# Four order tables of a fused decoder's attention rewritten: scan and C product of a side state-space model, the next context's normalising and turning, and the spacing of the key maxima

## The chip, the cores and the metric

The kernel runs on 1 core of one Trainium2 chip. Times are device microseconds (us) of one execution; the lower the better. The core's engines run side by side and meet at semaphores: TensorE (PE in the profile), VectorE (DVE), ScalarE (ACT), GpSimd (POOL) and SyncE (SP), which here only issues DMAs.

## The reference

A decoder layer on `x` (4 batches of 512 rows, 256 wide) with a context `ctx_1024` (4 batches of 1601 rows, 256 wide), in three steps, each followed by a layer norm over the sum with its input:

```python
# step 1, a Mamba block: 512 inner channels, 16 states each
dt = softplus(dt @ W_dt.T + b_dt)
dA = exp(dt[..., None] * A)
dBx = dt[..., None] * Bm[:, :, None, :] * xs[..., None]
def step(h, inputs):
    dA_t, dBx_t, C_t = inputs
    h = dA_t * h + dBx_t                      # the scan over 512 positions
    return h, einsum('bdn,bn->bd', h, C_t)    # the C product
out = (ys + xs * D) * silu(z) @ W_out.T
# step 2, cross attention: 16 heads of 64, keys and values from the context and the rows
xn, ln = layer_norm(ctx_1024), layer_norm(x)
q = ln @ Wq;  k, v = split(concat([xn, ln]) @ Wkv)       # 1601 + 512 = 2113 keys
out = softmax(q k^T / 8) v @ Wout
# step 3, a mixture of 8 experts (2 of them per row) and 2 shared ones
```

## The kernel before

Three blocks run one after the other: `mamba`, `attention`, `experts`. The change touches `attention` alone, about 450 to 2909 us of the profiled span. `mamba` finishes step 1 for one batch only. For the other three it keeps in DRAM what the scans need: `dtu` (dt and dt*x of 128 channels), `bc` (one row of B and one of C for each state), `y` and `z`. Their scans are done beside the attention of the batch before.

**Heads and slots.** `attention` goes through 4 batches of 16 heads, 64 heads `g`, and each head through KT = 17 slots `kt` of 128 keys. A slot on PE is two matmuls for the scores (L1246, L1247), then whatever the table gives it, then the product with the values of three slots before (LAG = 3, L1259). ACT takes the exponential of each slot's scores (L904). There are two banks of scores, so the engines walk through the slots nearly in step.

**The table.** `beside(g)` (L466) writes, for each head and slot, a list of letters with what is done beside it. PE, DVE, ACT and POOL each walk the same table in the same order and do their part of each letter; nothing but the semaphores holds an engine back. In the order in which a slot's list is filled:

- D and H: the scans. A batch has NU = 64 units, one for each block of 128 channels and state. Unit `u` has its D in slot `int(u * 2.85)`, counted through the batch's heads, and its H some slots `later`. At D, ACT makes the decays (L882) and POOL `dbx` = dtu * B (`times_b`, L795). At H, DVE scans (L992), and POOL multiplies with C (`times_c`, L802) and adds to `y` (L806).
- Q, K, V: projections; a head pair's Q and five K in slots 0 to 5 of its odd head (`g % 4` is 1 or 3); V in slots 6 to 15 of every fourth head.
- O: the output projection of the head before, in slots 6 to 9.
- P and G (head 12 of a batch): the output of the state-space block of the next batch (PE L1210) and the variance of its norm; J (head 13): that norm applied (DVE L1073).
- S, A, L, N, T: the next batch's context. S takes statistics of 13 tiles of 128 rows (head 12, DVE), A sums them in two halves, L does the same for the 512 rows of `x` (DVE L966 to L971), POOL makes the two `rstd` (L779, L782). N(i) normalises a pair of tiles on DVE (L983). T(i) turns it: PE transposes (L1137), ACT scales and shifts (L852) and copies (L856), DVE subtracts (L1008). `PREP` has 10 such pieces: six pairs and a single of context, a pair and two singles of `x`.
- X and M: the maxima of the next head's scores. X has 17 pieces, one matmul of 512 keys each (L1188) and one DVE reduction (L1042), in two banks: PE may be two pieces ahead of DVE. M turns the row of maxima (L1199) in slot 15.

**Buffers of the scans.** `dbx`, `decay`, `state` and `bc` have two buffers, by the unit's number `n`; `seen` has one. SP walks the slots too, with its loads in a fixed order. The load of `bc` for unit n waits until the C product of unit n - 2 has read its buffer:

```python
            def load_bc(b, u):
                n = unit(b, u)
                if n >= 2:
                    sp.wait_ge(seen_ready, n - 1)
                sp.dma_start(bc[:, n % 2]...,
                             KEPT["bc"][BATCHES[b], u % NS].partition_broadcast(P)).then_inc(bc_loaded[n % 2], 16)
```

It is 512 KB. The other loads of SP (weights, `wo`, the copies `k_one` of the keys) stand between these in the same queue.

Of the kernel before, what the change touches and what calls it, by code (L numbers as in the profile page):

```python
# [438 lines left out]
H, DH, LC = 16, 64, 1601  # L439
# [6 lines left out]
KT = -(-KV // P)  # L446
KL = KV - (KT - 1) * P
CTX_T = -(-LC // P)
# [10 lines left out]
NX = TT * (len(KC) - 1) + 1  # L459
# [6 lines left out]
def beside(g):  # L466

    at = {kt: [] for kt in range(KT)}
    b, h = divmod(g, H)
    j, more, following = g % HG, g + 1 < NH, b + 1 < B
    if following:
        for u in range(NU):
            for kind, later in (("D", 0), ("H", 2)):
                if divmod(int(u * U_STEP) + later, KT)[0] == h:
                    at[(int(u * U_STEP) + later) % KT].append((kind, b + 1, u))  # L480
    if j == 0:
        for i in range(V_EARLY, len(VB)):
            at[i - V_EARLY].append(("V", g // HG, i))
    if j % 2 == 1 and more:
        at[0].append(("Q", (g + 1) // 2, 0))
        for i in range(len(KC)):
            at[1 + i].append(("K", (g + 1) // 2, i))
    if j == HG - 1 and more:
        for i in range(V_EARLY):
            at[6 + 2 * i if i < 5 else 15].append(("V", (g + 1) // HG, i))  # L490
    if g > 0:
        for t in range(TT):
            at[6 + t].append(("O", g - 1, t))
    if following and h == 12:
        for t in range(TT):
            at[10 + t].append(("P", b + 1, t))
        at[15].append(("G", b + 1, 0))
        for t in range(CTX_T):
            at[t].append(("S", b + 1, t))
    if following and h == 13:  # L500
        at[3].append(("J", b + 1, 0))
        for i in range(2):
            at[7 + 4 * i].append(("A", b + 1, i))
        at[14].append(("L", b + 1, 0))
    if following and h == 14:
        for i in range(len(PREP)):
            at[(3 * i) // 2].append(("N", b + 1, i))
            at[1 + (3 * i) // 2].append(("T", b + 1, i))
    if b > 0 and h == 0:
        at[12].append(("E", b - 1, 0))  # L510
        at[16].append(("F", b - 1, 0))
    if more:
        for i in range(NX):
            at[i * 14 // NX if j % 2 == 0 else 3 + i * 11 // NX].append(("X", g + 1, i))
        at[15].append(("M", g + 1, 0))
    return at


BESIDE = [beside(g) for g in range(NH)]
BEFORE = [("S", 0, t) for t in range(CTX_T)] + [("A", 0, i) for i in range(2)] + [("L", 0, 0)]  # L520
BEFORE += [("N", 0, i) for i in range(3)]
# [9 lines left out]
POW = {x: i for i, x in enumerate(x for x in MADE if x[0] in "EGL" or x[0] == "A" and x[2] == 1)}  # L531


def attention(nc, ctx_rows, g1, b1, g2, b2, wq, wkv, wo, x1):
    w_dram = nc.dram_tensor("a_w_split", (NG, P, 6 * KD * GW), F32, kind="Internal").ap()

    with ExitStack() as ctx:
# [3 lines left out]
        def sem(name):  # L541
            return ctx.enter_context(nc.semaphore(name))
# [76 lines left out]
        rstd_ready = sem("a_rstd_ready")  # L619
# [33 lines left out]
        def x1_rows(b, t):  # L653
            return x1[:, BATCHES[b] * TT + t]
# [273 lines left out]
        def _(dve):  # L928
# [44 lines left out]
            def normalised(what):  # L973
                b, i = what[1:]
                t, n, r, col = PREP[i]
                if i == 0:
                    dve.wait_ge(rstd_ready, POW["L", b, 0] + 1)
                for j in range(t, t + n):
                    if j < CTX_T:
                        src = dst = rows[0:r, j]  # L980
                    else:
                        src, dst = x1_rows(b, j - CTX_T), lat[:, j - CTX_T]
                    s = nc.vector.tensor_scalar(dst, src, mv[0:r, j, 0:1], rstd[0:r, j:j + 1], ALU.subtract, ALU.mult)  # L983
                s.then_inc(rows_ready, 1)
# [92 lines left out]
            def make(what):  # L1077
                kind = what[0]
                if kind in "QKV":
                    low(what)  # L1080
                elif kind == "X":
                    row_max(what[1], what[2])
                elif kind == "O":
                    add_out(what)
                elif kind == "S":
                    row_stats(what)
                elif kind == "A":
                    row_sums(what)
                elif kind == "N":
                    normalised(what)  # L1090
                elif kind == "T":
                    low_rows(what)
                elif kind == "H":
                    scan(*what[1:])
                elif kind == "P":
                    add_mamba(what)
                elif kind == "L":
                    latent_sums(what[1])
                elif kind == "G":
                    norm_var(what[1], [("P", what[1], t) for t in (TT - 2, TT - 1)])  # L1100
                elif kind == "J":
                    norm_rows(what[1], ("G", what[1], 0))
                elif kind == "E":
                    norm_var(what[1], [("O", what[1] * H + H - 1, t) for t in (TT - 2, TT - 1)])
                elif kind == "F":
                    norm_rows(what[1], ("E", what[1], 0))
# [893 lines left out]
```

## Time and profile before

| | |
|---|---|
| median of 3 runs | 3380.14 us (3371.8 to 3387.71) |
| profiled execution | 3382.36 us, its span 3380.6 us |
| mean granted TensorE clock | 0.951 |
| busy: PE, DVE, ACT, POOL | 3017.8, 1940.5, 1351.0, 964.5 us |
| the attention's first head starts | about 461 us |
| first heads of batches 1, 2, 3 | about 1083, 1707, 2336 us |

The chain of work that ended last reaches back only to about 2909 us, into the experts, so it says nothing of the attention. There one reads stretches: the fourth batch has the same heads as the others without the scans and without a next context, so that its heads, beside those of another batch, show what these cost. The times at which heads begin are the starts of the score matmuls (L1247).

### The profile page before, as it was taken

Reading aid. Unit: us, or ns where it says so; the run is one execution under the profiler, and the core shown is the slowest. Engines: PE = TensorE matmul, PEld = TensorE weight load, DVE = VectorE, ACT = ScalarE, POOL = GpSimd, SP = SyncE. Lnnn points to the kernel's source line nnn. Section 1 sums busy time; section 2 is a strip of 40 time slices with the busy share of each in tenths; the row PEclk is TensorE's granted clock in tenths of the full one; section 3 lists DMA queues with packets and bytes.
Section 4 is the critical chain, followed back from the end, with each engine's and each line's share of the span. In section 5 each row is a group of like instructions: output and inputs, shape, how many; then the busy total and the mean of one; then the engine's idle time right before and its main releaser. Section 6 shows DMA issues by size and latency. Waiting matters only on the chain. (4 is left out here: it accounts for less than half of the span.)

```text
span 3380.6 us, 34291 instructions
## 1 busy us (share of the span) xinstructions
PE 3017.8 (89%) x11694; PEld 1872.9 (55%) x11694; DVE 1940.5 (57%) x3342; ACT 1351.0 (40%) x2320; POOL 964.5 (29%) x760
## 2 busy tenths in 40 slices
PE   6746289999999999999899999989999999799976
PEld 2212155665656565656566565656566665576655
DVE  4699466666555766665576666555555454442225
ACT  4532134445344445443544544344433434211111
POOL 1044336566101656540046666000000000102131
PEclk8878589999999999999999999999999999799997
DMA  3200344344112434231123433110111100411121
GB/s 114 89 0 0 130 127 129 103 126 132 39 35 63 129 100 134 95 104 34 51 86 125 126 104 115 33 35 14 35 22 33 42 13 13 156 55 54 50 59 37
DMA packets 90914, 248.57 MB, mean 74 GB/s; under 512 B 10660, under 2 KB 44584, under 8 KB 83064
## 3 DMA queue, kind: packets, MB, share of 16 engines
q1 hardware_dynamic: 86760, 237.04, 22.8%
q0 software_dynamic: 3408, 9.31, 1.0%
q8 instruction: 97, 1.59, 0.2%
q14 instruction: 73, 0.60, 0.1%
q10 hardware_dynamic: 576, 0.04, 0.0%
HBM read 183.34 MB, written 28.38 MB: 63 GB/s over the span
## 5 line engine op out<-in xcount | busy, mean ns | idle before, releaser
L904 ACT ACTIVATE a_p<-a_st 128x512 f32<-128x512 f32 (+1 forms) x1088 | 649.2, 597 | 1214.2 <-PE a_st L1247 1205.3
L1259 PE MATMUL a_o<-a_p,a_vals 128*65 128x512 f32 (+1 forms) x2176 | 1118.4, 596 | 0.0
L1042 DVE TENSOR_REDUCE a_maxes<-a_mx 128x1 f32<-128x512 f32 x1024 | 673.3, 682 | 112.3 <-PE a_mx L1188 106.0
L1246 PE MATMUL a_st<-a_qd,a_kodd 128*128 128x512 f32 (+1 forms) x544 | 434.7, 799 | 0.0
L1246 PE MATMUL a_st<-a_qd,a_keven 128*128 128x512 f32 (+1 forms) x544 | 434.6, 799 | 0.0
L1247 PE MATMUL a_st<-a_qm,a_kone 65*128 65x512 f32 (+1 forms) x1088 | 431.8, 397 | 0.0
L802 POOL TENSOR_TENSOR a_shared<-a_shared,a_bc 128x512 f32<-128x512 f32 x192 | 245.5, 1279 | 477.7 <-DVE a_shared L992 477.7
L1259 PEld LDWEIGHTS a_o<-a_p,a_vals 128*65 128x65 f32 (+1 forms) x2176 | 288.6, 137 | 124.5 <-issue 2.7
L1247 PEld LDWEIGHTS a_st<-a_qm,a_kone 65*128 65x128 f32 (+1 forms) x1088 | 204.1, 188 | 265.5 <-issue 265.4
L992 DVE TENSOR_TENSOR_SCAN a_shared<-a_shared 128x512 f32<-128x512 f32 x192 | 234.3, 1220 | 178.8 <-POOL a_shared L795 129.6
L795 POOL TENSOR_TENSOR a_shared<-a_dtu,a_bc 128x512 f32<-128x512 f32 x192 | 245.1, 1276 | 197.7 <-DMA a_bc<-m_kept_bc 197.7
L784 POOL TENSOR_TENSOR a_erstd<-a_emv,a_half 128x4 f32<-128x4 f32 x7 | 7.1, 1014 | 919.8 <-DVE a_emv L1068 919.6
L1144 PE MATMUL a_ring<-a_kvh,a_wt 128*128 128x512 f32 (+1 forms) x768 | 228.6, 380 | 26.7 <-POOL a_wt L820 20.7
L806 POOL TENSOR_TENSOR a_y<-a_y,a_shared 128x512 f32<-128x512 f32 x192 | 245.0, 1276 | 15.3
L1188 PE MATMUL a_mx<-a_keven,a_qd 128*128 128x512 f32 x512 | 215.3, 471 | 32.9 <-DVE a_maxes L1042 28.6
L1188 PE MATMUL a_mx<-a_kodd,a_qd 128*128 128x512 f32 x512 | 218.8, 452 | 28.9 <-DVE a_maxes L1042 28.3
L1035 DVE COPY a_vals<-a_ring 128x512 f32<-128x512 f32 (+2 forms) x160 | 97.6, 610 | 235.8 <-PE a_ring L1144 234.9
L1246 PEld LDWEIGHTS a_st<-a_qd,a_kodd 128*128 128x128 f32 (+1 forms) x544 | 101.7, 187 | 160.2 <-issue 118.7
L1246 PEld LDWEIGHTS a_st<-a_qd,a_keven 128*128 128x128 f32 (+1 forms) x544 | 101.7, 187 | 159.2 <-issue 103.9
L1144 PEld LDWEIGHTS a_ring<-a_kvh,a_wt 128*128 128x128 f32 x768 | 142.3, 192 | 67.1 <-issue 21.1
L1523 ACT ACTIVATE e_silu<-e_h 128x512 f32<-128x512 f32 x71 | 42.4, 597 | 334.5 <-PE e_h L1865 185.5
L1651 DVE TENSOR_TENSOR e_gate<-e_silu,e_h 128x512 f32<-128x512 f32 x71 | 48.7, 686 | 220.5 <-ACT e_silu L1523 217.3
(242 smaller groups left out, 4451.6 us busy)
## 6 DMA issues: line engine op xcount, KB each, us to landing
a_bc<-m_kept_bc SPq DMA_DIRECT2D x192, 512.0 KB, 3.7
a_wt<-a_w_split SPq DMA_DIRECT2D x15, 1536.0 KB, 9.4
a_kone<-a_keven SPq DMA_DIRECT2D x32, 528.5 KB, 5.0
a_kone<-a_kodd SPq DMA_DIRECT2D x32, 528.5 KB, 5.5
e_wall<-in_w_t_dram SPq DMA_DIRECT2D x27, 512.0 KB, 5.2
a_shared<-in_ctx_dram SPq DMA_DIRECT2D x4, 1536.0 KB
a_w_split<-a_wt SPq DMA_DIRECT2D x4, 1536.0 KB, 6.5
a_dtu<-m_kept_dtu SPq DMA_DIRECT2D x12, 512.0 KB, 4.9
```

Of the source, the lines that this page charges most:

```text
L795: nc.gpsimd.tensor_tensor(dbx[:, n % 2], dtu[:, c % 2, 1], bc[:, n % 2, 0], ALU.mult).then_inc(dbx_ready, 1)
L802: nc.gpsimd.tensor_tensor(seen, state[:, n % 2], bc[:, n % 2, 1], ALU.mult).then_inc(seen_ready, 1)
L806: nc.gpsimd.tensor_tensor(y[:, c], y[:, c], seen, ALU.add).then_inc(y_added, 1)
L904: nc.scalar.activation(p[0:r, s % 4], st[0:r, s % 2], ACT.Exp, scale=SCALE).then_inc(exp_done, 1)
L992: nc.vector.tensor_tensor_scan(state[:, n % 2], decay[:, n % 2], dbx[:, n % 2], 0.0, ALU.mult, ALU.add).then_inc(scanned, 1)
L1035: o = nc.vector.tensor_copy(vals[0:r, t * HG:(t + w) * HG, 0:DH], made)
L1042: nc.vector.reduce_max(maxes[:, c, t:t + 1], mx[:, i % 2], AX_X).then_inc(mx_max, 1)
L1144: mm = nc.tensor.matmul(out, x(k), y(k), start=(j == 0), stop=(j == len(terms) - 1))
L1188: mm = nc.tensor.matmul(mx[:, i % 2], qd[of(g)][:, t * P:(t + 1) * P], kk[:, c * 512:(c + 1) * 512], start=True, stop=True)
L1246: nc.tensor.matmul(st[0:r, s % 2], keys_of(g)[:, kt * P:kt * P + r], qd[of(g)][:], start=True, stop=False)
L1247: nc.tensor.matmul(st[0:r, s % 2], k_one[g % 2][0:DH + 1, kt * P:kt * P + r], qm[of(g)][0:DH + 1, :], start=False, stop=True).then_inc(st_ ...
L1259: nc.tensor.matmul(ps_o[0:DH + 1, g % 2], vals[0:r, kt * HG + j, :], p[0:r, s % 4], start=(kt == 0), stop=(kt == KT - 1)).then_inc(pv_done, 1)
```

## The change

Four things, all in the tables. H comes four slots behind D, where it was two. A's halves move from slots 7 and 11 of head 13 to slot 10 of head 12 and slot 0 of head 13, L from slot 14 to slot 13. N and T, all in head 14 before, are spread over heads 13 and 14, each T two slots behind its N, where it was one. In odd heads the 17 pieces of X are spaced wider at first and end one slot later.

```diff
-            for kind, later in (("D", 0), ("H", 2)):
+            for kind, later in (("D", 0), ("H", 4)):
                 if divmod(int(u * U_STEP) + later, KT)[0] == h:
                     at[(int(u * U_STEP) + later) % KT].append((kind, b + 1, u))
...
+        at[10].append(("A", b + 1, 0))
     if following and h == 13:
+        at[0].append(("A", b + 1, 1))
         at[3].append(("J", b + 1, 0))
-        for i in range(2):
-            at[7 + 4 * i].append(("A", b + 1, i))
-        at[14].append(("L", b + 1, 0))
-    if following and h == 14:
+        at[13].append(("L", b + 1, 0))
+    if following and h in (13, 14):
         for i in range(len(PREP)):
-            at[(3 * i) // 2].append(("N", b + 1, i))
-            at[1 + (3 * i) // 2].append(("T", b + 1, i))
+            for kind, slot in (("N", 6 + 2 * i), ("T", 8 + 2 * i)):
+                if i >= CTX_T // 2 + 1:
+                    slot += 1
+                if slot // KT == h - 13:
+                    at[slot % KT].append((kind, b + 1, i))
...
-            at[i * 14 // NX if j % 2 == 0 else 3 + i * 11 // NX].append(("X", g + 1, i))
+            at[i * 14 // NX if j % 2 == 0 else 3 + i if i < 2 else 5 + (i - 2) * 2 // 3].append(("X", g + 1, i))
...
                 if i == 0:
+                    dve.wait_ge(rstd_ready, POW["A", b, 1] + 1)
+                if t == CTX_T:
                     dve.wait_ge(rstd_ready, POW["L", b, 0] + 1)
```

The first place is POOL's order at the start of a batch's scans; in the kernel before, where L795 is `times_b`, L802 and L806 are `times_c`:

```order
L795 TENSOR_TENSOR a_shared<-a_dtu,a_bc 128x512 [waits a_bc_loaded0,a_dtu_loaded0,a_turned_low]
L802 TENSOR_TENSOR a_shared<-a_shared,a_bc 128x512 [waits a_scanned]
L806 TENSOR_TENSOR a_y<-a_y,a_shared 128x512 [waits a_seen_ready,a_y_loaded]
L795 TENSOR_TENSOR a_shared<-a_dtu,a_bc 128x512 [waits a_bc_loaded1,a_turned_low]
L802 TENSOR_TENSOR a_shared<-a_shared,a_bc 128x512 [waits a_y_added,a_scanned]
L806 TENSOR_TENSOR a_y<-a_y,a_shared 128x512 [waits a_seen_ready]
L795 TENSOR_TENSOR a_shared<-a_dtu,a_bc 128x512 [waits a_scanned,a_bc_loaded0]
```

The same start in the changed kernel, where the three lines are L798, L805 and L809:

```order
L798 TENSOR_TENSOR a_shared<-a_dtu,a_bc 128x512 [waits a_bc_loaded0,a_dtu_loaded0,a_turned_low]
L798 TENSOR_TENSOR a_shared<-a_dtu,a_bc 128x512 [waits a_bc_loaded1,a_turned_low]
L805 TENSOR_TENSOR a_shared<-a_shared,a_bc 128x512 [waits a_scanned]
L809 TENSOR_TENSOR a_y<-a_y,a_shared 128x512 [waits a_seen_ready,a_y_loaded]
L798 TENSOR_TENSOR a_shared<-a_dtu,a_bc 128x512 [waits a_scanned,a_bc_loaded0]
L805 TENSOR_TENSOR a_shared<-a_shared,a_bc 128x512 [waits a_y_added,a_scanned]
L809 TENSOR_TENSOR a_y<-a_y,a_shared 128x512 [waits a_seen_ready]
L798 TENSOR_TENSOR a_shared<-a_dtu,a_bc 128x512 [waits a_scanned,a_bc_loaded1]
```

Before, the three operations of one unit stand together, B(0) C(0) B(1) C(1) B(2). Now it is B(0) B(1) C(0) B(2) C(1) B(3): the C product of unit n - 2, which lets SP load `bc` for unit n, stands directly ahead of that unit's product with B.

The second place is DVE's order at the next context's pieces, early in head 14, in the kernel before (L983 is N, L1008 the end of T, L1042 an X):

```order
L1042 TENSOR_REDUCE a_maxes<-a_mx 128x1 [waits a_mx_full] x2
L1008 TENSOR_TENSOR a_kvl<-a_shared,a_kvh 128x2x256 [waits a_turned_high]
L983 TENSOR_SCALAR a_shared<-a_shared,a_mv,a_rstd 128x256 x2
L1042 TENSOR_REDUCE a_maxes<-a_mx 128x1 [waits a_mx_full]
L1008 TENSOR_TENSOR a_kvl<-a_shared,a_kvh 128x2x256 [waits a_turned_high]
L1042 TENSOR_REDUCE a_maxes<-a_mx 128x1 [waits a_mx_full]
L983 TENSOR_SCALAR a_shared<-a_shared,a_mv,a_rstd 128x256 x2
```

DVE's order in slots 10 to 15 of head 13 in the changed kernel, where N is L988, the end of T is L1013, X is L1047 and L1049, and L969 to L974 are the statistics of the rows of `x` (L):

```order
L1013 TENSOR_TENSOR a_kvl<-a_shared,a_kvh 128x2x256 [waits a_turned_high]
L988 TENSOR_SCALAR a_shared<-a_shared,a_mv,a_rstd 128x256 x2
L1047 TENSOR_REDUCE a_maxes<-a_mx 128x1 [waits a_mx_full]
L969 BN_STATS a_stats<-rows 128x6 x4
L972 BN_AGGR a_mv<-a_stats 128x2 [waits a_dve_step]
L972 BN_AGGR a_mv<-a_stats 128x2 x3
L974 TENSOR_SCALAR a_mv<-a_mv 128x4 [waits a_dve_step]
L1047 TENSOR_REDUCE a_maxes<-a_mx 128x1 [waits a_mx_full] x2
L1013 TENSOR_TENSOR a_kvl<-a_shared,a_kvh 128x2x256 [waits a_turned_high]
L988 TENSOR_SCALAR a_shared<-a_shared,a_mv,a_rstd 128x256 x2
L1049 TENSOR_REDUCE a_maxes<-a_mx 128x4 [waits a_mx_full]
```

Before, each N stood right behind the end of the T of the pair before it and one slot ahead of its own T on PE. Now a slot or two with X lie between, and the last maxima of head 13 stand behind L and behind a T and an N.

## Rows read from the trace of the kernel before

**Rows 1.** The page: busy time, share of the span and instructions of each engine.

```profile
PE 3017.8 (89%) x11694; PEld 1872.9 (55%) x11694; DVE 1940.5 (57%) x3342; ACT 1351.0 (40%) x2320; POOL 964.5 (29%) x760
```

**Rows 2.** Windows, heads 0-9, batches 1, 3: us, busy PE PEld DVE ACT POOL, clock, DMA.

```profile
1082.80:1457.70 374.90, 362.06 (x1415) 221.32 (x1414) 255.88 (x416) 185.01 (x320) 227.60 (x181) 1.00 0.37 113
2335.60:2696.50 360.90, 357.83 (x1415) 223.04 (x1414) 186.83 (x357) 149.20 (x260) 1.01 (x1) 1.00 0.12 31
```

**Rows 3.** Page, costliest groups: times_c on POOL and the scan on DVE.

```profile
L802 POOL TENSOR_TENSOR a_shared<-a_shared,a_bc 128x512 f32<-128x512 f32 x192 | 245.5, 1279 | 477.7 <-DVE a_shared L992 477.7
...
L992 DVE TENSOR_TENSOR_SCAN a_shared<-a_shared 128x512 f32<-128x512 f32 x192 | 234.3, 1220 | 178.8 <-POOL a_shared L795 129.6
```

**Rows 4.** Line L992, one window for each batch's 64 scans: first and last start.

```profile
L992 DVE TENSOR_TENSOR_SCAN a_shared<-a_shared x64: 1211/1223/1227, 465.7 to 856.0; 128x512 f32<-128x512 f32 x64
...
L992 DVE TENSOR_TENSOR_SCAN a_shared<-a_shared x64: 1208/1223/1226, 1088.1 to 1483.4; 128x512 f32<-128x512 f32 x64
...
L992 DVE TENSOR_TENSOR_SCAN a_shared<-a_shared x64: 1208/1223/1226, 1712.1 to 2109.0; 128x512 f32<-128x512 f32 x64
```

**Rows 5.** Timeline of POOL: start, length, line, idle before.

```profile
630.10 1.28 POOL L795 TENSOR_TENSOR a_shared<-a_dtu,a_bc 128x512 f32<-128x512 f32 x1
632.77 1.28 POOL L802 TENSOR_TENSOR a_shared<-a_shared,a_bc 128x512 f32<-128x512 f32 x1 [1.39 <-DVE a_shared L992]
...
635.37 1.26 POOL L795 TENSOR_TENSOR a_shared<-a_dtu,a_bc 128x512 f32<-128x512 f32 x1
```

**Rows 6.** Page, DMA issues: KB each, median us to landing.

```profile
a_bc<-m_kept_bc SPq DMA_DIRECT2D x192, 512.0 KB, 3.7
```

**Rows 7.** Tile a_bc: loads issued at 478.9, at 839.2, and all of batch 0's scans.

```profile
DMA to landing us min/median/max: 5.3/5.3/5.3
...
DMA to landing us min/median/max: 6.1/6.1/6.1
...
DMA to landing us min/median/max: 3.3/3.7/10.2
```

**Rows 8.** Timeline of SP near the 62nd unit: start, length of issuing.

```profile
828.71 0.32 SPq L690 DMA_DIRECT2D a_bc<-m_kept_bc  x1
829.07 0.43 SPq L736 DMA_DIRECT2D a_wt<-a_w_split  x1
...
833.97 5.58 SPq L690 DMA_DIRECT2D a_bc<-m_kept_bc  x2
```

**Rows 9.** Timeline of POOL at the 62nd unit.

```profile
844.21 1.26 POOL L795 TENSOR_TENSOR a_shared<-a_dtu,a_bc 128x512 f32<-128x512 f32 x1 [3.65 <-DMA a_bc<-m_kept_bc]
```

**Rows 10.** Waits of the whole span: PE for the maxima.

```profile
PEld a_mx L1188 <- DVE a_maxes L1042: 88.0, 123, 3.8
...
PE a_mx L1188 <- DVE a_maxes L1042: 56.9, 89, 3.4
```

**Rows 11.** Waits in slots 3 to 5 of head 11 of batch 3.

```profile
PEld a_mx L1188 <- DVE a_maxes L1042: 1.1, 2, 0.7
...
PE a_mx L1188 <- DVE a_maxes L1042: 0.5, 2, 0.3
```

**Rows 12.** Waits in head 14 of batch 0.

```profile
PE a_ring L1137 <- DVE a_shared L983: 7.4, 8, 1.8
```

**Rows 13.** Windows: heads 13, 14 of batch 0, 13 of batch 1, 13, 14 of batch 3.

```profile
951.10:993.30 42.20, 40.42 (x138) 24.57 (x137) 25.60 (x67) 18.64 (x33) 3.43 (x2) 0.92 0.19 57
993.30:1036.50 43.20, 34.70 (x136) 19.04 (x135) 23.26 (x51) 25.46 (x49) 0.00 (x0) 1.00 0.06 13
1578.50:1617.30 38.80, 37.03 (x137) 22.55 (x136) 25.61 (x67) 18.63 (x33) 3.44 (x2) 1.00 0.20 62
2804.00:2841.90 37.90, 37.29 (x137) 22.67 (x137) 20.67 (x38) 18.63 (x33) 0.00 (x0) 1.00 0.07 15
2841.90:2870.70 28.80, 28.80 (x101) 16.45 (x100) 13.62 (x26) 11.21 (x19) 0.00 (x0) 1.00 0.09 19
```

**Rows 14.** Line L966 in head 13 of batch 0.

```profile
L966 DVE BATCH_NORM_STATS2 a_stats<-rows x4: 408/408/416, 988.5 to 989.5; 128x6 f32<-128x256 f32 x4
```

## The prediction

> **What bounds the kernel now.** I began with the page's busy times: PE is busy 89% of the span, more than any other [rows 1]. The chain that ended last lies in the experts, which the change leaves alone, so for the attention I compared stretches. Heads 0 to 9 take 374.9 us in batch 1, with scans beside them, and 360.9 us in batch 3, without; PE is busy for all but 3.1 us of the latter [rows 2]. So PE sets the pace, and the scans cost 14.0 us in these ten heads. Without scans a slot takes 360.9 / 170 = 2.12 us, and the 2.85 slots from one unit to the next 6.05 us.
>
> The scans have a ring of their own. POOL waits 477.7 us for the scan, 192 times, and DVE 129.6 us for POOL [rows 3]. The reader is to see how the ring closes where it is tight: POOL multiplies with B from 630.10 to 631.38, waits 1.39 us while DVE scans, multiplies with C at 632.77, adds, and begins with the next B at 635.37 [rows 5]. One unit takes 5.27 us there, less than 6.05, so the ring holds PE up only in heads whose slots are short. Over whole batches the scans start 390.3, 395.3 and 396.9 us apart from first to last [rows 4], 6.20 to 6.30 us a unit.
>
> **Scan and C product four slots behind.** No instruction is added or removed; the ring is cut open. DVE no longer scans right behind POOL's B: the scan of unit n stands behind B(n + 1) on POOL, so the 1.39 us in which POOL waits for it can go. That is the gain meant, at most the 14.0 us above, or 15 a batch with the units that fall behind head 9 (64 units at 2.85 slots end in head 10).
>
> Now what comes late next. `bc` has two buffers; SP loads unit n's when C(n - 2) has read it. Before, POOL did C(n - 2), add, B(n - 1), C(n - 1), add and then B(n), so a load had over 6 us. Now C(n - 2), its add and B(n) are neighbours: a load has 1.28 us of cover, the add. POOL is in order, so C(n - 1) stands behind the waiting B(n), and C(n - 1) is what lets SP load for unit n + 1. This is a new ring, one unit long, with a DMA in it: C, load, B, C, load, B. DVE's next scan waits for B, the maxima (X) stand behind that scan on DVE, and PE, two maxima ahead at most, waits for them; ACT's decays, and the exponentials behind them, wait for the scan too. The wait is not new in kind. It shows once in batch 0: a load issued at 833.97 [rows 8] lands 10.2 us later, the longest of batch 0 [rows 7], and POOL, which would have gone on at 840.6, sits idle for 3.65 us and starts B at 844.21, 0.07 us behind the landing [rows 9].
>
> Its length: C 1.28 and B 1.28 [rows 3, 5], 0.14 us between the operations (0.07 behind a landing as just seen, 0.07 for the two others, C to SP's issue and B to C), and the load. The page gives 3.7 us in the median for 512 KB [rows 6], and the shortest in batch 0 is 3.3 [rows 7]. A ring adds up means, not medians: of 62 loads in batch 0 (from unit 2 on), 14 land after 4.3 us or more, the first 5.3 (issued at 478.9), the last 6.1 (issued at 839.2), 5.81 on average, and 48 after 3.62 on average [rows 7]: together 4.11. Batches 1 and 2 give the same to 0.02. The long ones have a cause that stays: SP issues key copies and weights right behind a `bc` load, as at 829.07 behind 828.71 [rows 8]. So a unit takes 2.56 + 0.14 + 4.11 = 6.81 us, above today's 6.20 to 6.30.
>
> This is a floor, whatever PE does: from scan 0 to scan 63 it is scan 1.22, 0.07, C 1.28, load 4.14 with its issue, 0.07 to B(2), 61 units of 6.81, and B(63) with its hand-over 1.37, in all 423.6 us. Against 390.3, 395.3 and 396.9 that is +33.3, +28.3 and +26.7, together +88. At the end of each batch PE may be two light slots (28.8 / 17 = 1.7 us each [rows 13]), some 3 us, ahead of the waiting scan, which I count as not yet so today: -9. Sum **+79**. Both ends: with every load at 3.62 the stretch is 393.2 us, the sum about 0 and with the lead -10; with a mean of 4.4 it is 18 us a batch more than taken, +132. I take 4.11, since the companions of the long loads stay in the queue where they are.
>
> **A rule against a row.** The rows say 3.3 at best and 3.7 in the median for this load [rows 6, 7]. The Trainium skill, DMA: Bandwidth & Descriptors (Anatomy of one DMA) fits a DMA as about 2.0 us fixed plus bytes / 436 GB/s, fitted on GpSimd's path, which for 512 KB would be an estimate of 3.2 us and a unit of 5.9: below the pace of PE, and the ring would cost nothing. This case's trace does not agree, with 3.7. The same page (Rules for kernel authors) says to issue early and wait late; this edit brings issue and wait closer, and by that rule it speaks against the change.
>
> **Maxima spaced wider in odd heads.** PE waits for maxima 88.0 + 56.9 us in the whole span (weight loads and matmuls) [rows 10]; part is the scans' doing. In slots 3 to 5 of an odd head, where the keys' subtractions crowd DVE, it is 1.1 + 0.5 = 1.6 us [rows 11]. Two maxima in slots 3 and 4 each become one, with two in slot 5. There the second has to wait for the maximum of slot 4, which stands behind the fourth key chunk on DVE: of the 1.6 I count half, 0.8 us. It counts only where POOL does not set the pace: heads 11, 13, 15 in three batches and seven heads of batch 3, 16 heads, **-13**. Bounds: 0, and 1.6 each, -26. The last maximum, a slot later, still lies a slot ahead of M.
>
> **The next context.** Head 14 takes 43.2 us against 28.8 in batch 3, head 13 42.2 and 38.8 against 37.9 [rows 13]. Of this, PE waits 7.4 us in head 14 for the normalised rows, 8 times [rows 12]; the rest are transposes, which are only moved, and DVE waits. With T two slots behind N these waits should go: -22 in three batches. In batch 0 head 13 shows a clock of 0.92 and 3.4 us more than in batch 1 at 1.00: one dip to the 1.2 GHz level behind the stall at J. Fewer maxima beside J may spare it in some batches: -3. Costs: L, 4 statistics of 0.41 us and what follows, about 2.1 us on DVE [rows 14], now stands ahead of two maxima in slot 13, and the last maximum and M behind it, and behind the end of a T, which waits for ACT; five T now fall in the odd head 13, whose DVE has more to do. I count 4 us a batch, +12. The halves of A go where DVE is busy 25.6 of 42.2 us [rows 13]: nothing, and some 1 us if that cover were gone. Sum **-13**. Bounds -30 and +5.
>
> **Sum.** 79 - 13 - 13 = +53, on the profiled execution's own 3382.4 us: 3435. The median of the runs is 2.2 us lower, so **3433**.
>
> **Rivals.**
> - *The POOL ring with the load in it decides*, as above: +53. For it: the buffers and the order; against it: the load has only been seen while POOL was busy. Mean loads of 4.0 to 4.35 give 3413 to 3477. Chance 0.72.
> - *The long loads fall into slack* and only the usual 3.62 counts: -10 - 26 = -36, 3344. For it: where slots take over 2.4 us (6.81 / 2.85), POOL catches up; against it: light ones use this up again, since the ring is over the average pace. 0.10. Between this and the first, near 3380, 0.06. The time turns at a mean load of about 3.83 us, where the scans' term is +26.
> - *The edit does what it seems made for*: the scans' stalls vanish, 15 us a batch, and the maxima help in all 31 odd heads at 0.8, -45 - 25 - 13 = -83, 3299. That needs a unit under 6.05 us, a load under 3.35, which the fastest alone reach; the page cited above would have it so. 0.04.
> - *Slower still*: loads grow when SP's other transfers bunch behind the later issue, or POOL waits for scans as well. A mean of 4.6 gives +90 more, 3523. 0.08.
>
> **Range and chances.** 3390 to 3480 holds the first case and edges of its neighbours, and leaves out about 2 in 10. What differs by under 0.5% (17 us) counts as the same. Faster 0.14, same 0.06, slower 0.80.
>
> **What would show it.** In the changed profile POOL's `times_b` should wait for `a_bc` often, over 100 times and over 400 us in total, and its wait for the scan should be small. The scans' first and last starts should lie about 424 us apart. Heads 0 to 9 should be slower than 374.9 us, near 400. Heads 11 and 15 should be 0.8 us shorter, 13 and 14 together a few us. PE's wait for L983's successor should be near nothing. I am wrong if the load takes under 3.8 us on average, or if POOL finds `bc` there already.

## The result, and the profile after

| | before | after |
|---|---|---|
| median | 3381.02 us (4 runs) | 3462.21 us (4 runs, 3461.65 to 3465.95) |
| ratio | | 1.0234 [1.0216, 1.0251] |
| span of the profiled execution | 3380.6 us | 3460.8 us |
| mean granted TensorE clock | 0.951 | 0.941 |

The change costs 81 us; 53 were forecast. In the changed kernel the product with B is L798, the product with C L805, the addition L809, the scan L997, N L988, the end of T L1013, X L1193 on PE and L1047 on DVE. The page's busy times, to be read beside [rows 1]:

```profile
PE 3038.6 (88%) x11690; PEld 1885.5 (54%) x11694; DVE 2034.7 (59%) x3342; ACT 1351.4 (39%) x2320; POOL 1040.8 (30%) x760
...
L798 POOL TENSOR_TENSOR a_shared<-a_dtu,a_bc 128x512 f32<-128x512 f32 x192 | 253.5, 1321 | 585.7 <-DMA a_bc<-m_kept_bc 565.8
L997 DVE TENSOR_TENSOR_SCAN a_shared<-a_shared 128x512 f32<-128x512 f32 x192 | 330.9, 1723 | 113.8 <-POOL a_shared L798 68.8
...
L809 POOL TENSOR_TENSOR a_y<-a_y,a_shared 128x512 f32<-128x512 f32 x192 | 313.4, 1632 | 15.3
...
L805 POOL TENSOR_TENSOR a_shared<-a_shared,a_bc 128x512 f32<-128x512 f32 x192 | 244.8, 1275 | 99.6 <-DVE a_shared L997 99.2
```

Two things are to be seen. POOL's idle time has changed sides: it waited 477.7 us for scans [rows 3], and now waits 99.2 us for scans and 565.8 us for `bc`. In each kernel three long waits of either kind stand at the start of a batch. Inside the batches POOL waited 418 us for scans and 18 for `bc`; now it waits 31 for scans and 394 for `bc`. And with no instruction added, DVE is busy 94 us longer and POOL 76: the scan takes 1.72 us instead of 1.22, the addition 1.63 where POOL's other operations take 1.28 to 1.32. The first was forecast, the second not. How often POOL waited, in the view of waits (total us, times, longest):

```profile
POOL a_shared L798 <- DMA a_bc<-m_kept_bc: 565.8, 179, 71.5
...
POOL a_shared L805 <- DVE a_shared L997: 99.2, 25, 25.4
```

Before, the wait for `bc` was 197.7 us in 12 times, nine of them inside the batches. The scans of the three batches, one window each, with the number, min/median/max in ns, and first and last start, against [rows 4]:

```profile
L997 DVE TENSOR_TENSOR_SCAN a_shared<-a_shared x64: 1210/1830/2303, 468.6 to 888.9; 128x512 f32<-128x512 f32 x64
...
L997 DVE TENSOR_TENSOR_SCAN a_shared<-a_shared x64: 1210/1598/2319, 1122.2 to 1540.7; 128x512 f32<-128x512 f32 x64
...
L997 DVE TENSOR_TENSOR_SCAN a_shared<-a_shared x64: 1210/1715/2243, 1775.6 to 2196.2; 128x512 f32<-128x512 f32 x64
```

They are 420.3, 418.5 and 420.6 us apart, where the ring was worked out at 423.6: 30.0, 23.2 and 23.7 more than before, 76.9 in all. The windows of heads 0 to 9 of batches 1 and 3, heads 13 and 14 of batch 0 and head 13 of batch 3, with the columns of [rows 2, 13]:

```profile
1112.30:1506.80 394.50, 370.77 (x1416) 226.79 (x1415) 282.03 (x416) 185.61 (x320) 242.36 (x177) 0.97 0.34 106
2419.60:2780.20 360.60, 355.68 (x1416) 223.06 (x1415) 187.24 (x357) 149.20 (x260) 1.01 (x1) 1.00 0.12 31
980.80:1032.30 51.50, 42.00 (x158) 25.11 (x157) 30.31 (x73) 25.34 (x47) 3.44 (x2) 0.97 0.17 49
1032.30:1066.00 33.70, 31.57 (x115) 17.42 (x114) 18.20 (x39) 18.29 (x36) 0.00 (x0) 1.00 0.06 13
2887.60:2925.30 37.70, 36.72 (x137) 22.65 (x136) 20.78 (x38) 18.64 (x33) 0.00 (x0) 1.00 0.07 15
```

Heads 0 to 9 with scans take 394.5 us instead of 374.9; without them nothing moved. Head 13 has become 9.3 us longer and head 14 9.5 shorter. By the starts of the score matmuls, summed over heads:

| us | batch 0 | batch 1 | batch 2 | sum of the differences | forecast |
|---|---|---|---|---|---|
| heads 0 to 10, before | 404.4 | 410.1 | 411.7 | | |
| heads 0 to 10, after | 433.9 | 434.8 | 436.8 | +79.3 | +79 |
| heads 11, 15 and all of batch 3 | | | | 0 | -13 with head 13 |
| head 13, before / after | 42.1 / 51.5 | 38.8 / 53.1 | 42.1 / 51.5 | +33.1 | |
| head 14, before / after | 43.2 / 33.7 | 43.2 / 33.8 | 43.2 / 33.8 | -28.3 | |
| heads 13 and 14 | | | | +4.8 | -13 |

Batch 3 begins at 2419.6 us instead of 2335.6, 84 later; what follows gives 3 back.

### The profile page after: what moved, and what is told of

Same layout as the page of the kernel before. It is cut to its first block and busy times, and to the rows that moved or that the text cites. A ratio compares the mean times of both kernels' runs of the same rounds, so it can differ in the third digit from the quotient of the medians.

```text
span 3460.8 us, 34287 instructions
## 1 busy us (share of the span) xinstructions
PE 3038.6 (88%) x11690; PEld 1885.5 (54%) x11694; DVE 2034.7 (59%) x3342; ACT 1351.4 (39%) x2320; POOL 1040.8 (30%) x760
## 5 line engine op out<-in xcount | busy, mean ns | idle before, releaser
L1264 PE MATMUL a_o<-a_p,a_vals 128*65 128x512 f32 (+1 forms) x2176 | 1136.3, 604 | 0.0
L1047 DVE TENSOR_REDUCE a_maxes<-a_mx 128x1 f32<-128x512 f32 x1024 | 676.1, 682 | 126.0 <-PE a_mx L1193 120.5
L798 POOL TENSOR_TENSOR a_shared<-a_dtu,a_bc 128x512 f32<-128x512 f32 x192 | 253.5, 1321 | 585.7 <-DMA a_bc<-m_kept_bc 565.8
L997 DVE TENSOR_TENSOR_SCAN a_shared<-a_shared 128x512 f32<-128x512 f32 x192 | 330.9, 1723 | 113.8 <-POOL a_shared L798 68.8
L809 POOL TENSOR_TENSOR a_y<-a_y,a_shared 128x512 f32<-128x512 f32 x192 | 313.4, 1632 | 15.3
L1193 PE MATMUL a_mx<-a_keven,a_qd 128*128 128x512 f32 x512 | 223.3, 472 | 68.7 <-DVE a_maxes L1047 68.7
L805 POOL TENSOR_TENSOR a_shared<-a_shared,a_bc 128x512 f32<-128x512 f32 x192 | 244.8, 1275 | 99.6 <-DVE a_shared L997 99.2
L1193 PE MATMUL a_mx<-a_kodd,a_qd 128*128 128x512 f32 x512 | 223.8, 463 | 41.9 <-DVE a_maxes L1047 41.6
L1226 PE MATMUL a_ring<-a_wo,a_osb 65*128 65x257 f32 x512 | 158.3, 392 | 22.9 <-DVE rows L1061 22.2
L1149 PE MATMUL a_ring<-a_wt,a_kvh 128*128 128x256 f32 (+1 forms) x1088 | 175.4, 283 | 0.0
```

Source lines behind the costliest of these rows:

```text
L798: nc.gpsimd.tensor_tensor(dbx[:, n % 2], dtu[:, c % 2, 1], bc[:, n % 2, 0], ALU.mult).then_inc(dbx_ready, 1)
L805: nc.gpsimd.tensor_tensor(seen, state[:, n % 2], bc[:, n % 2, 1], ALU.mult).then_inc(seen_ready, 1)
L809: nc.gpsimd.tensor_tensor(y[:, c], y[:, c], seen, ALU.add).then_inc(y_added, 1)
L997: nc.vector.tensor_tensor_scan(state[:, n % 2], decay[:, n % 2], dbx[:, n % 2], 0.0, ALU.mult, ALU.add).then_inc(scanned, 1)
L1047: nc.vector.reduce_max(maxes[:, c, t:t + 1], mx[:, i % 2], AX_X).then_inc(mx_max, 1)
L1149: mm = nc.tensor.matmul(out, x(k), y(k), start=(j == 0), stop=(j == len(terms) - 1))
```

## The experiments

The theory: the loss is POOL's ring with the load of `bc` in it, and what closes it is two buffers of `bc`. The rivals: the distance of H from D as such; scans and POOL's products slowing each other; heads 13 and 14. Each kernel but one, which ran once, was timed beside the kernel before on the same chip. That kernel's median was 3379.2 to 3382.9 us in these sets, so a difference between kernels of two sets is good to some 4 us.

**A third buffer of `bc` in the changed kernel.** Nothing else is touched: the load waits for the C product of unit n - 3.

```diff
-        bc = sb("a_bc", [P, 2, 2, S])
+        bc = sb("a_bc", [P, 3, 2, S])
...
-                if n >= 2:
-                    sp.wait_ge(seen_ready, n - 1)
-                sp.dma_start(bc[:, n % 2]...
+                if n >= 3:
+                    sp.wait_ge(seen_ready, n - 2)
+                sp.dma_start(bc[:, n % 3]...
```

> The changed kernel with three buffers for bc instead of two: the load for unit n waits for the C product of unit n - 3, so that a whole unit of POOL's work lies between that product and the B product that needs the load. Theory 1 (a ring of C product, load and B product on POOL sets the pace): POOL's 565.8 us of waiting for a_bc, 179 times, shrink to the three batch starts, heads 0 to 10 of a batch fall from 434 to 437 us to under 410, and the kernel takes 3345 us, between 3320 and 3375. Theory 2 (scan and POOL's products slow one another when they run at once, 1.72 us for a scan instead of 1.22 in the changed kernel, and that alone makes it slow): nothing of the overlap is taken away, and it stays within 20 us of 3462.

Measured: 3346.36 us, 0.9891 [0.9876, 0.9905] of before, 116 us below the changed kernel. The waits of POOL and the window of heads 0 to 9 of batch 1:

```profile
POOL a_shared L805 <- DVE a_shared L997: 404.4, 134, 25.9
POOL a_shared L798 <- DMA a_bc<-m_kept_bc: 197.0, 16, 70.5
```

```profile
1072.20:1438.80 366.60, 357.48 (x1415) 221.90 (x1414) 267.77 (x416) 185.18 (x320) 236.01 (x179) 1.00 0.38 118
```

The waits for `bc` fall from 179 to 16 (inside the batches from 394 us to 27), and the ten heads from 394.5 to 366.6 us, 8 below the kernel before and 6 above the heads without scans. The order on POOL and DVE is the changed one; so the two buffers are what makes the order dear. Scans and POOL's products still run side by side (a scan takes 1.44 us on average), so their overlap is not what made the loss.

**The scans' table alone, on the kernel before.**

```diff
-            for kind, later in (("D", 0), ("H", 2)):
+            for kind, later in (("D", 0), ("H", 4)):
```

> The kernel before with H four slots behind D and nothing else changed. The prediction's term is +79: 3382 + 79 = 3461 by theory 1, between 3440 and 3480, with the scans' first and last starts about 420 us apart in each batch. If the other edits matter for it, it lies elsewhere: were the loss that of the context pieces and the maxima, this kernel would be at or under 3400.

Measured: 3460.85 us, 1.0222 [1.0207, 1.0237]. The one number makes 78 of the 81 us (the median of before was 3382.93 beside it); the other edits together make about nothing. Its POOL:

```profile
POOL a_shared L795 <- DMA a_bc<-m_kept_bc: 571.9, 178, 75.8
```

**Three slots instead of two or four**, again on the kernel before (`("H", 3)`).

> The kernel before with H three slots behind D. In about six of seven units POOL's order is still B(n) C(n), in the others B(n + 1) stands ahead of C(n); the scan is one slot later in all. Theory 1 (the order on POOL decides, with two bc buffers): near the kernel before, 3370 to 3395. Rival (the distance in slots decides: whatever is late grows with it): half way to the 3461 of four slots, near 3420.

Measured: 3373.23 us, 0.9974 [0.9959, 0.9989].

```profile
POOL a_shared L802 <- DVE a_shared L992: 414.6, 166, 22.4
POOL a_shared L795 <- DMA a_bc<-m_kept_bc: 244.0, 37, 75.8
```

D comes every 2.85 slots. At three slots H falls behind the next D only where that D comes after two slots instead of three, about one unit in seven; POOL waits for `bc` 37 times. At four slots it falls behind always. So it is not the distance that costs, but that on POOL the order B(n), C(n - 1) has taken the place of C(n - 1), B(n).

**The next context alone**, on the kernel before: A, L, N and T as in the change, nothing else.

> The kernel before with only the A, L, N and T pieces in their new slots. The prediction's term was -13. The profile of the changed kernel shows head 13 at 51.5 to 53.1 us (38.8 to 42.1 before) and head 14 at 33.7 (43.2 before), which is +5 for three batches: 3387 by that reading, 3369 by the prediction. If the loss in head 13 came from scans that ran late, head 13 would be near 45 here and the time near 3365; there are no scans in head 13, so I expect 51 to 53 us again.

Measured: 3388.61 us (10 runs), 1.0016 [1.0005, 1.0027], +5.7. Head 13 takes 51.5, 54.2, 51.5 us and head 14 33.7 to 33.8, as in the changed kernel. The gain in one head is lost in the other.

**The maxima's spacing alone**, on the kernel before.

> The kernel before with only the maxima of odd heads spaced wider. The prediction's term was -13, and -25 where POOL does not set the pace. The changed kernel's profile shows odd heads of batch 3 at 37.8 and 46.3 us as before, so that the wait in slots 3 to 5 has only moved to slot 5 (3.71 us instead of 2.65). By that reading the time is within 5 us of 3381; by the prediction 3356 to 3368.

Measured: 3375.34 us (10 runs), 0.9978 [0.9969, 0.9987], -7.6. The heads that show the spacing undisturbed, the odd ones of batch 3, became shorter by about 0.1 us at most (37.8 and 46.3). The rest is scattered: head 13 takes 39.3, 39.2, 40.9 for 42.1, 38.8, 42.1, which is mostly the dip of the granted clock that batches 0 and 2 had there. So the interval lies below 1, but by another way than the one that I priced.

**A third buffer in the kernel before.** This asks how much of the 116 us is the ring that the change made, and how much a third buffer brings in any order. The edit is that of the first experiment.

> The kernel before with three buffers for bc and nothing else: the control of e1_bc3. In the order B(n) C(n) a load has over 6 us of cover already, and the ring of 5.27 us per unit (B product, scan, C product, add) has no load in it. Theory 1: within 10 us of 3383, the one long wait near the 62nd unit of each batch gone at most. If a third buffer helped for another reason than the ring of the changed kernel, this kernel would come down as e1_bc3 did, by 30 us and more.

Measured: 3355.48 us, 0.9930 [0.9912, 0.9947], -24.5, where next to nothing was expected. Its POOL waits, and the windows of its heads 10 and 13 of batch 0:

```profile
POOL a_shared L802 <- DVE a_shared L992: 477.0, 192, 21.3
POOL a_shared L795 <- DMA a_bc<-m_kept_bc: 180.0, 3, 75.7
```

```profile
829.70:861.30 31.60, 29.56 (x101) 16.17 (x100) 18.85 (x31) 13.54 (x23) 19.94 (x16) 1.00 0.30 80
946.90:985.70 38.80, 37.04 (x138) 22.58 (x137) 25.62 (x67) 18.64 (x33) 3.44 (x2) 1.00 0.21 62
```

The 12 waits for `bc` of the kernel before are now 3, and those 3 are the ones ahead of a batch. What is gone is nine waits, 17.7 us in all, one or two a batch of them longer than 1 us, as the 3.65 us behind the load of 10.2 us [rows 7, 9], and what followed. Head by head, up to head 14 of the last batch, the granted clock is 1.00, the level of 2.4 GHz, where head 10 of every batch, head 13 of two and head 2 of one had shown 0.92 to 0.95; head 10 takes 31.6 us for 35.3, head 13 of batch 0 38.8 for 42.2 [rows 13]. Of the 26 us between the two profiles 18.5 lie in heads 0 to 10 and 6.6 in head 13, where POOL waits for no load: its dip of the clock varies between the batches of one kernel (0.92 in two, 1.00 in the third), and that the buffer took it away is not shown. Of the 116 us, then, some 25 come in the order of before too; the other 90 are the change's. And with three buffers the changed kernel (0.9891 [0.9876, 0.9905]) is faster than the kernel before (0.9930 [0.9912, 0.9947]): taken together, the changed tables do bring something, about 12 us, once the loads have cover.

**Half the load, in the changed kernel.** Only the B row is loaded, 256 KB; the C product multiplies with B's row, so this kernel leaves C out of its result.

```diff
-                sp.dma_start(bc[:, n % 2].rearrange("p i s -> p (i s)"),
-                             KEPT["bc"][BATCHES[b], u % NS].partition_broadcast(P))...
+                sp.dma_start(bc[:, n % 2, 0],
+                             KEPT["bc"][BATCHES[b], u % NS, 0:S].partition_broadcast(P))...
...
-                nc.gpsimd.tensor_tensor(seen, state[:, n % 2], bc[:, n % 2, 1], ALU.mult)...
+                nc.gpsimd.tensor_tensor(seen, state[:, n % 2], bc[:, n % 2, 0], ALU.mult)...
```

> The changed kernel with bc loads of 256 KB: only the row of B is loaded, and the C product multiplies with that row too, so the C product leaves out the row of C. Order, buffers and instructions are the same; only the load in the ring is shorter. Theory 1: a unit is 2.70 us plus the load. The load of 512 KB took 3.92 us on average; should 256 KB take 3.2, a unit is 5.9 us, under PE's 6.05, and the time falls by 61 units x 3 batches x 0.6 us and somewhat more, to 3350 to 3380. Theory 2 (scan and POOL's products slow one another): the overlap stays, and with it 3440 to 3462.

Measured: 3424.76 us, 1.0131 [1.0112, 1.0151]. A miss in size: -37 against the changed kernel, where -80 to -110 was expected.

```profile
DMA to landing us min/median/max: 3.0/3.2/8.7
```

```profile
POOL a_shared L798 <- DMA a_bc<-m_kept_bc: 495.2, 177, 69.3
```

```profile
POOL a_shared L805 <- DVE a_shared L997: 137.9, 44, 26.6
```

Half the bytes took only 0.5 us off the median (3.7 before) and 0.43 off the mean, 3.48. The ring is then 2.70 + 3.48 = 6.18 us, still above the 6.05 of the slots alone. And units came 6.43 to 6.55 us apart. Added up over the 186 units of the ring, the loads took 80 us less; the products with B took 13 us more (they stretch where a scan runs beside them); and POOL, inside the batches, waited 67 us for scans instead of 31. The ring is confirmed, but it was not a lever of 1:1: what the loads gave back went in part to the next thing to come late, the scan.

**POOL's two other operations cut to copies, in the changed kernel.** The C product becomes a copy of the state, the addition a copy; this leaves the product and the sum over states out. It ran once, so its time has no interval.

```diff
-                nc.gpsimd.tensor_tensor(seen, state[:, n % 2], bc[:, n % 2, 1], ALU.mult)...
+                nc.gpsimd.tensor_copy(seen, state[:, n % 2])...
...
-                nc.gpsimd.tensor_tensor(y[:, c], y[:, c], seen, ALU.add)...
+                nc.gpsimd.tensor_copy(y[:, c], seen)...
```

> The changed kernel with POOL's two operations behind the scan made copies of one input: the C product is left out (seen is a copy of the state) and the sum over states too (y is a copy of seen). A look at durations alone. In the changed kernel a scan takes 1.22 us alone and 2.1 us beside C product and add, while the add behind it takes 2.1 us instead of 1.28. If the two engines take turns at a way into SBUF only when POOL reads two inputs, scans beside the copies take 1.22 us; if any operation of POOL does it, they stay at 1.7 us and more. I expect the former to hold in part: the mean scan under 1.5 us.

Measured: 3414.43 us. The page's groups:

```profile
L997 DVE TENSOR_TENSOR_SCAN a_shared<-a_shared 128x512 f32<-128x512 f32 x192 | 267.4, 1393 | 80.7 <-POOL a_shared L798 40.4 <-issue 39.1
L809 POOL COPY a_y<-a_shared 128x512 f32<-128x512 f32 x192 | 160.2, 834 | 11.9
L805 POOL COPY a_shared<-a_shared 128x512 f32<-128x512 f32 x192 | 117.3, 611 | 161.3 <-DVE a_shared L997 161.2
```

The scan's mean falls from 1.72 to 1.39 us, but does not return to 1.22: beside the copies a scan takes 1.50 on average, and alone 1.22 (beside a product with B, which is still there, also 1.50). The copy into `y` takes 0.83 on average, 0.62 with no scan beside it. So operations of one input slow the scan too, for a shorter time. The ring is 0.67 us shorter here as well, so that the 48 us below the changed kernel are no price of the overlap alone.

**The next context, cut another way**, on the kernel before: N alone goes a slot earlier, the first to slot 16 of head 13; all T stay in head 14.

```diff
+        at[16].append(("N", b + 1, 0))
     if following and h == 14:
...
-            at[(3 * i) // 2].append(("N", b + 1, i))
+            if i > 0:
+                at[(3 * i) // 2 - 1].append(("N", b + 1, i))
```

> The kernel before with the context pieces turned in head 14 as before, T in its old slots, and only N moved one slot ahead, so that it stands two slots or more before its T. A, J and L stay. If the loss of the changed kernel's head 13 comes from five T in a head whose DVE is full (each T on DVE waits for ACT, and the maxima behind it), and the gain of its head 14 from N being early, then head 13 stays at 38.8 to 42.1 us and head 14 falls from 43.2 us by most of the 7.4 us for which PE waits for N: to 36 to 38 us. Time 3360 to 3370. If N early does nothing, head 14 stays at 43 and the time at 3383.

Measured: 3366.49 us, 0.9964 [0.9950, 0.9978], -13.5. Head 14 takes 37.4 us for 43.2, head 13 40.4 in every batch (38.8 to 42.1 before).

**What these point to, together**: the changed kernel with three buffers of `bc`, H four slots behind, the wider maxima, and the context of the last experiment in place of the change's.

> What the experiments point to, together: three bc buffers, H four slots behind D, the maxima spaced wider, and the context pieces of e7_ctx14 (T in head 14 as before, N a slot earlier) in place of the changed kernel's. From e1_bc3's profile, heads 13 and 14 are 83.6, 85.4 and 86.7 us; in e7_ctx14 they are 77.8 in each batch. That is 22 us less: 3346 - 22 = 3324, between 3310 and 3335. If the heads 13 and 14 of e1_bc3 were long because of scans and clock rather than of the five T in head 13, they stay near 84 and the time near 3346.

Measured: 3321.77 us, 0.9830 [0.9814, 0.9847], 57 us below the kernel before and 140 below the changed one. POOL's waits (the scans are L996 here):

```profile
POOL a_shared L804 <- DVE a_shared L996: 400.0, 132, 25.9
POOL a_shared L797 <- DMA a_bc<-m_kept_bc: 194.1, 15, 69.2
```

**The same with H three slots behind.**

> e8_best with H three slots behind D: scan and POOL's products overlap less (scans of 1.30 us on average in e6_scan3, 1.44 in e1_bc3). If the overlap costs more than the fourth slot brings, this is the faster one, by up to 10 us; if the distance carries the light heads, e8_best is, by about as much. I expect within 8 us of e8_best, on the slower side.

Measured: 3326.5 us, 0.9840 [0.9824, 0.9857]. The intervals overlap. The two ran on one chip, and three of the four times with three slots lie above all four with four (3320.6 to 3324.8): if the distance matters here, it is by 4 or 5 us in favour of four.

## Why the prediction was right in sign and short by 28 us

**Scan and C product: +79 forecast, +79.3 measured in heads 0 to 10.** Place, sign and mechanism are shown: alone it makes the loss (3460.85), a third buffer takes it away (3346.36), and POOL waits where the forecast says. The ring can be read off POOL's timeline (start, length, idle before):

```profile
481.18 1.28 POOL L798 TENSOR_TENSOR a_shared<-a_dtu,a_bc 128x512 f32<-128x512 f32 x1 [1.64 <-DMA a_bc<-m_kept_bc]
482.42 1.28 POOL L805 TENSOR_TENSOR a_shared<-a_shared,a_bc 128x512 f32<-128x512 f32 x1
483.77 2.08 POOL L809 TENSOR_TENSOR a_y<-a_y,a_shared 128x512 f32<-128x512 f32 x1
487.06 1.26 POOL L798 TENSOR_TENSOR a_shared<-a_dtu,a_bc 128x512 f32<-128x512 f32 x1 [1.22 <-DMA a_bc<-m_kept_bc]
```

From one B to the next it is 5.88 us: B, C, the load (issued at 483.72, landed at 487.00), B. The addition is the only cover that the load has; that it takes 2.08 us here costs the ring nothing.

That the two numbers agree to 0.3 us is luck: the terms behind them do not. The trace shows each. In all 186 units of the ring (from unit 2 on) POOL's B begins 0.07 us behind the landing of its load, so POOL never found `bc` there. From the C product of unit 0 to that of unit 62 the parts of the ring add up to:

| us, 62 units | forecast | batch 0 | batch 1 | batch 2 |
|---|---|---|---|---|
| loads, issue to landing | 254.8 | 241.1 | 242.0 | 244.3 |
| C and B products | 158.7 | 160.0 | 160.9 | 162.2 |
| from one to the next | 8.7 | 3.9 | 3.9 | 3.8 |
| POOL's waits for a scan | 0 | 13.2 | 9.4 | 8.4 |
| sum | 422.2 | 418.2 | 416.2 | 418.7 |

The term that was too long is the load. It was taken as 4.11 us "since the companions of the long loads stay in the queue where they are"; it was 3.89, 3.90 and 3.94, with 10 or 11 loads of 4.3 us or more where the kernel before had 13 or 14. The companions stay, but the loads of `bc` come later between them: 9 of the 186 were issued while another transfer was under way, where it had been 37. That this is why they are shorter is likely, not tested. With 3.91 us and all else as forecast the scans' term would have been +42 and the time near 3396. The term that was missing is the wait for a scan, which the forecast had at nothing: 31 us in three batches, most of it in heads 3 and 7, the longest ones with scans (46.3 us each before, which is 7.8 us for the 2.85 slots of a unit): there PE's pace, not the ring, sets when the next scan comes. Stretched B products (1.32 us on average in batch 1) make 8 more. The lead of PE at the batch's end, -9, was not found: the heads grew by 79.3 where the scans' stretch grew by 76.9. "I am wrong if the load takes under 3.8 us on average": it stayed above by 0.1.

**The maxima: -13 forecast, 0 where it was to show.** The step that failed is "Two maxima in slots 3 and 4 each become one ... I count half, 0.8 us". In the odd heads of batch 3 slots 3, 4, 5 took 3.20, 4.07, 2.65 us and take 2.96, 2.93, 3.71: of the 1.4 us that leave slots 3 and 4, 1.1 come back in slot 5 and the rest, but for 0.1, in the slots behind. Heads 11 and 15 and the odd heads of batch 3 became shorter by 0.1 us at most. The 1.6 us that were halved were too much from the start: they add the wait of the weight load and that of its matmul, which are the same stall. PE itself stood idle for 0.61 us in each of these odd heads, and 0.98 after the change. [rows 2] had the bound: 3.1 us idle in ten heads, five of them odd. Spacing work wider within a head whose DVE is short of time moves the wait; the work of the head is the same. The 7.6 us that the edit brought alone came from heads with scans and from fewer dips of the clock, and in the changed kernel it can't be seen apart.

**The next context: -13 forecast, +4.8 measured.** The gain is there, and near its size: in head 14 PE's wait for N fell from 7.4 to 0.2 us a batch, and its whole idle time (length less busy) from 8.5 to 2.1, 19 us in three batches where 22 were forecast. The other 9 of the 28.3 us that head 14 lost are transposes, which went to head 13. The step that failed is "five T now fall in the odd head 13, whose DVE has more to do. I count 4 us a batch": PE's idle time there rose from 1.8 to 9.5 us in every batch, 23 us in three. The waits in head 13 of batch 0 (window 980.8 to 1032.3):

```profile
DVE a_kvl L1013 <- ACT a_kvh L859: 8.1, 4, 3.0
PE a_mx L1193 <- DVE a_maxes L1047: 7.6, 4, 2.2
...
PEld a_mx L1193 <- DVE a_maxes L1047: 6.8, 4, 2.5
```

The chain reads from bottom to top; the last two lines are the same stalls, once at the weight load and once at its matmul. PE's matmuls wait 7.6 us for maxima there, against 1.7 in this head before, and 1.6 more at the turning of the row of maxima. DVE, in order, stands with the maxima behind L1013, the end of a T, which waits 8.1 us for ACT's copy, and ACT has 47 operations in this head for 33. T is not a matter of DVE's time but of a hand-over PE to ACT to DVE, and in an odd head the maxima and the keys stand behind it. In head 14, where there are fewer, the same hand-over costs little, and moving only N, as one experiment did, gets 13.5 us.

**The clock and the rest.** The mean granted clock fell from 0.951 to 0.941. By head, the changed kernel shows 0.91 to 0.92 in head 2 and 0.87 to 0.88 in head 10 of each batch, 0.91 to 0.97 in several others; the kernel before had 1.00 in all but six of the first 63 heads. In heads 0 to 10 PE stands at the 1.2 GHz level for 34, 34 and 31 us a batch, where it had been 3, 3 and 7. These dips come with stalls of the ring: in head 10 of batch 0 POOL waits 6.15 us for a load, PE then sits idle for 6.95 us until 878.95, and from 875.2 the clock is at 1.2 GHz for 10.2 us. The forecast had none of it. How much of the +79.3 the dips make is not settled, but it is bounded: no load, product or hand-over in the table above waits for PE, so inside the scans' stretch a slower PE can only be behind the 31 us in which POOL waited for scans. Why the dips fall in heads 2 and 10 above all stays open. Of the 28 us missing, then, none is the scans' term: 13 are the maxima and 18 the context, less the 3 that came back after them.

**The page on DMA.** The fit of the Trainium skill, DMA: Bandwidth & Descriptors (Anatomy of one DMA) would have given an estimate of 3.2 us for 512 KB, and 2.6 for 256 KB; it is a fit of transfers that GpSimd issues, and these are SyncE's. The runs show 3.7 and 3.2 in the median: the difference between them, 0.5 us, agrees with the page's 0.6, the fixed part does not. By that estimate the change would have cost nothing; the rows were right to go by.

## What to carry to other kernels

Before moving a consumer further behind its producer on an in-order engine, write down that engine's order and ask which release starts a load, and what stands between the release and the load's use: the number of buffers has to grow with the distance, or an engine that was waiting for compute waits for DMA. Here the distance in slots meant little in itself: with a unit every 2.85 slots, three slots hardly changed the order and four turned it over everywhere. When such a ring closes, its period is the sum of the means, late loads included, and of what else its engine waits for in the long heads. A third buffer is worth asking for even where the mean load has cover (24.5 us here). Price a moved step by every hand-over in it, in the head it is moved to, not by its own busy time. And take what a stall of PE can give back from PE's idle time in the window: the waits at weight loads and at matmuls, added, count it twice.

## What the runs showed that I had not expected

**The scan on DVE and a product on POOL slow each other.** In the kernel before none of the 192 scans lay beside a POOL operation of the scans, and each took 1.22 us. In the changed kernel 38 lie alone (1.22 us), 36 beside a B only (1.52), 37 beside an addition only (1.66) and 81 beside a C product and an addition (2.08). The two engines' timelines at one such place, POOL first:

```profile
548.35 1.27 POOL L805 TENSOR_TENSOR a_shared<-a_shared,a_bc 128x512 f32<-128x512 f32 x1
549.70 2.07 POOL L809 TENSOR_TENSOR a_y<-a_y,a_shared 128x512 f32<-128x512 f32 x1
```

```profile
548.47 2.23 DVE L997 TENSOR_TENSOR_SCAN a_shared<-a_shared 128x512 f32<-128x512 f32 x1 [0.27 <-issue]
```

The C product had begun 0.12 us before the scan and runs at its usual 1.27 us; the scan takes 1.0 us more than alone; then the addition, begun while the scan still ran, takes 0.8 more than alone. From the C product's start to the addition's end it is 3.42 us, near the 3.77 that the three take one after the other (1.27, 1.22, 1.28). It looks as if they take turns, and whichever began first goes on at its full speed; the lengths show this, what the engines take turns at they do not. The kernel with copies shows the same, shorter (POOL's timeline, then DVE's):

```profile
485.89 0.61 POOL L805 COPY a_shared<-a_shared 128x512 f32<-128x512 f32 x1
486.57 1.43 POOL L809 COPY a_y<-a_shared 128x512 f32<-128x512 f32 x1
```

```profile
486.04 1.54 DVE L997 TENSOR_TENSOR_SCAN a_shared<-a_shared 128x512 f32<-128x512 f32 x1 [1.43 <-POOL a_shared L798]
```

The Trainium skill, GPSIMD Engine Reference (Specifications) says that GpSimd shares its SBUF interfaces with VectorE and that they contend with DVE instructions of two SBUF inputs, which the scan has. This agrees. The price in these traces is up to 1.1 us on a scan of 1.22 and 0.8 on the addition, and a POOL operation of one input is enough. I had the scan at 1.22 us in every case.

It costs little here. In the changed kernel's ring it makes the 8 us of the stretched B products; the addition is outside the ring; and with three buffers the scans still take 1.44 us on average in the first experiment, and that kernel is faster than the kernel before. In the kernel before, the tight coupling B, scan, C had kept the two apart.

**The price of a few late loads.** POOL waited for `bc` in only nine places inside the batches of the kernel before, 17.7 us in all (the worst load of batch 0 took 10.2 us [rows 7]), and the load's median is well covered. A third buffer, which took these waits away, still brought 24.5 of 3380 us. Some of the 24.5 is the lower clock that no longer followed a stall of PE; its share was not taken apart.
